# A key-value stack, code scalings and running sums: one DMA pass, five GpSimd steps and three VectorE steps put elsewhere in the order

## The reference

```python
# cross attention, on the layer-normed x; the first 257 context rows have weights of their own
q = rms_norm(linear(x, q_w, q_b), norm_q_w)
k = rms_norm(linear(context, k_w, k_b), norm_k_w)      # all further context rows
v = linear(context, v_w, v_b)
probs = softmax(einsum('bqhd,bkhd->bhqk', q, k) * scale)
out = linear(einsum('bhqk,bkhd->bqhd', probs, v), o_w, o_b)
# self attention: every weight is a product of codes and block scales
w = codes * jnp.repeat(scales, 32, axis=0)
```

## Time and profile before

| | us |
|---|---|
| median of 3 runs | 1200.07 (1199.26 to 1204.12) |
| the profiled execution | 1197.79 |
| its span, first to last instruction | 1196.1 |

### The profile page before, as it was taken

How to read it: one execution, slowest core, us unless ns; L and a number is a source line. 1 busy time by engine, 2 the same in 40 slices (tenths; PEclk the granted TensorE clock), 3 DMA queues, 4 the chain that set the end, 5 groups by cost and what they waited for, 6 DMA issues and landing times.

```text
span 1196.1 us, 26329 instructions
## 1 busy us (share of the span) xinstructions
PE 1154.2 (96%) x8794; PEld 950.5 (79%) x8794; DVE 947.6 (79%) x1611; ACT 876.7 (73%) x1891; POOL 764.0 (64%) x1064
## 2 busy tenths in 40 slices
PE   6999999999999999999999999999998879899998
PEld 4778888888888888888888888888887658588886
DVE  4778788887788787787878887778887778499997
ACT  5577877778777777777787777877777757388885
POOL 7988788887889788898887887888873000000000
PEclk9999999999999999999999999999999989899999
DMA  7135677665875657766667665686654899579990
GB/s 257 40 97 153 170 194 184 175 180 158 215 191 152 171 168 204 195 168 175 177 170 195 181 172 167 170 209 166 184 140 108 252 394 398 208 270 362 364 369 15
DMA packets 129327, 236.72 MB, mean 198 GB/s; under 512 B 15014, under 2 KB 42150, under 8 KB 128812
## 3 DMA queue, kind: packets, MB, share of 16 engines
q1 hardware_dynamic: 129196, 235.05, 66.5%
HBM read 140.87 MB, written 17.04 MB: 132 GB/s over the span
## 4 chain that ended last, share of the span: by engine, by line
PE 61%; POOL 11%; SPq 11%; DVE 6%; DMA 4%; issue 4%; ACT 2%; POOLq 0%; DVEq 0%; ACTq 0%
PE ps L1573 22%; PE ps L1437 12%; SPq L354 10%; PE ps L1599 5%; PE ps L1632 4%; DMA code_scale<-code_scales 3%; PE ps L1800 3%; PE ps L1803 3%; PE ps L1806 3%; POOL cx_blocks L624 2%; DVE small L1197 2%; POOL cx_blocks L622 2%; PE ps L1821 1%; PE ps L1829 1%; PE ps L1825 1%
## 5 line engine op out<-in xcount | busy, mean ns | idle before, releaser
L1573 PE MATMUL ps<-w_text,cx_blocks 128*128 128x512 f32 x1974 | 488.2, 394 | 0.5 <-ACT v_first L814 0.5
L1573 PEld LDWEIGHTS ps<-w_text,cx_blocks 128*128 128x128 f32 x1974 | 366.9, 188 | 86.8 <-issue 7.7
L857 ACT ACTIVATE p<-ps,small 128x512 f32<-128x512 f32 (+2 forms) x400 | 272.3, 682 | 116.7 <-DVE small L1199 112.8
L1197 DVE TENSOR_REDUCE small<-ps 128x1 f32<-128x512 f32 (+2 forms) x400 | 269.7, 674 | 87.4 <-PE ps L1599 86.9
L1437 PE MATMUL ps<-ident,p 128*128 128x128 f32 x1584 | 209.0, 273 | 11.0 <-DVE pt L1191 7.0
L1437 PEld LDWEIGHTS ps<-ident,p 128*128 128x128 f32 x1584 | 184.8, 141 | 41.2 <-issue 11.5
L839 ACT ACTIVATE pt<-ps 128x512 f32<-128x512 f32 (+1 forms) x296 | 164.4, 589 | 36.9 <-PE ps L1437 36.8
L622 POOL TENSOR_TENSOR cx_blocks<-cx_sum,small 128x256 fp32r<-128x256 f32 x188 | 119.1, 633 | 82.5 <-PE ps L1573 69.0
L624 POOL TENSOR_TENSOR cx_blocks<-cx_sum,cx_blocks 128x256 fp32r<-128x256 f32 x188 | 140.3, 746 | 14.7
L1599 PE MATMUL ps<-k_stack,q_stack 96*128 96x512 f32 (+1 forms) x400 | 146.2, 438 | 2.0 <-ACT p L857 1.7
L1199 DVE TENSOR_TENSOR small<-small 128x1 f32<-128x1 f32 x400 | 132.6, 331 | 13.7
(11 more groups left out here) (252 smaller groups left out, 1923.3 us busy)
## 6 DMA issues: line engine op xcount, KB each, us to landing
expert<-experts SPq DMA_DIRECT2D x34, 1536.0 KB, 8.7
k_stack<-kt_hi SPq DMA_DIRECT2D x384, 128.0 KB, 3.3
cx<-ctx_t SPq DMA_DIRECT2D x48, 512.0 KB, 5.0
k_stack<-kt_lo SPq DMA_DIRECT2D x192, 128.0 KB, 3.1
codes<-codes SPq DMA_DIRECT2D x64, 256.0 KB, 3.1
code_scale<-code_scales SPq DMA_DIRECT2D x64, 256.0 KB, 3.8
scaled<-codes SPq DMA_DIRECT2D x64, 256.0 KB, 2.3
weight_q<-scaled SPq DMA_DIRECT2D x1, 4096.0 KB, 15.3
```

Of the source, the lines that this page charges most:

```text
L857: eng.activation(pb[:, lo:hi], score_bank(s, h)[:, lo:hi], exp, bias=nm[1 - par][:, h:h + 1], accum_out=ls[1 - par][:, h:h + 1]).then_inc( ...
L1197: eng.tensor_reduce(ngm[:, h:h + 1], score_bank(s, h)[:, lo:hi], AX.X, ALU.max, negate=True).then_inc(e_gm, 1)
L1573: last = eng.matmul(ps_a[(p + i + 1) % 2][:, :], blk[:, i, a, c * P:(c + 1) * P], w_t[:, i, w, c * D:(c + 1) * D], start=(i in FRESH and c ...
```

## The change

- SyncE: the pass for tile C stands behind `stack(0)` instead of ahead of the load and `stack(0)`. In step 23 the last store moves with it; the wait for all stores stays behind it.
- GpSimd: scaling A comes after the third sum and block 4 of the first half, instead of ahead of them; scaling B after blocks 0 and 1 of the second half and the next group's first key norm, instead of ahead; scaling C at the end of the second half, instead of behind block 2. `key_norm(s, 3)` comes between the first and the second sum of the second half, instead of after both.
- VectorE: `scale_attention` is cut in two. In steps 2 to 23 the two steps on the sums run at the end of slot 1 and the rescaling at the end of slot 2, instead of both in slot 5. In the drained steps both stay where they were.

Nothing is added or removed.

```diff
@@ SyncE, step
-                pass_codes(s, 1, m, loop)
                 if 1 <= s < NG:
                     load_next(s)
                     eng.wait_ge(e_klo, s * GT + GT)
...
                     stack(0, False)
                     if not loop and s == NG - 1:
                         eng.dma_start(x_again[:, :], t["x"]).then_inc(e_xa, 16)
+                pass_codes(s, 1, m, loop)
                 if not loop and s == NG - 2:
                     for b in range(2):
                         eng.wait_ge(e_cs[b], 16 * (NW // 2))
@@ GpSimd, step
                 if strass:
                     split(0, 2, sum_y[:, :, :], 2)
                     split(0, 3, sum_x[:, :, :], 0)
+                    third_sum(0)
+                    split(0, 4, sum_x[:, :, :], 3)
                 scale_codes(s * W_STEP - (W_FIRST * W_STEP + 1), (m + 1) % 2, loop)
                 if strass:
-                    third_sum(0)
-                    split(0, 4, sum_x[:, :, :], 3)
                     fourth_sum(0)
                 if strass:
                     split(0, 5, sum_y[:, :, :], 4)
                 if nxt:
-                    first_sums(1)
+                    first_sum(1)
                 if cur:
                     key_norm(s, 3, 1)
+                if nxt:
+                    second_sum(1)
                 if strass:
                     split(0, 6, quarter(0, 1, 1), 0)
-                scale_codes(s * W_STEP - W_FIRST * W_STEP, m % 2, loop)
                 if nxt:
                     split_first(1)
                     if s > 0:
                         key_norm(s + 1, 0, 1)
                     if s == 0:
                         last_weight_sum()
+                scale_codes(s * W_STEP - W_FIRST * W_STEP, m % 2, loop)
+                if nxt:
                     split(1, 2, sum_y[:, :, :], 2)
-                scale_codes(s * W_STEP - (W_FIRST * W_STEP - 1), (m + 1) % 2, loop)
-                if nxt:
                     split(1, 3, sum_x[:, :, :], 0)
...
                     split(1, 6, quarter(1, 1, 1), 0)
+                scale_codes(s * W_STEP - (W_FIRST * W_STEP - 1), (m + 1) % 2, loop)
                 if s == NG - 1:
                     image_part()
@@ VectorE, slot and drain
-                    if end and j == 5:
+                    if end and s < NG - 1 and j == 1:
+                        scale_sums()
+                    if end and s < NG - 1 and j == 2:
                         scale_attention()
...
                     if end and h == 12:
+                        scale_sums()
                         scale_attention()
```

More of the change, by code:

```diff
@@ L629, in step @@
                 if strass:
-                    first_sums(0)
+                    first_sum(0)
+                    second_sum(0)
                 if cur:
```

6 lines of the change are left out of this document (4 added, 2 removed).

## The result

The changed kernel takes 1226.67 us, the median of 4 runs (1222.94 to 1232.08). Four runs of the kernel before on the same chip have a median of 1199.66 us (1198.69 to 1204.12). The ratio is 1.0221 with a 95% interval of 1.0175 to 1.0267: the kernel became 2.2% slower, where 0.5% faster was forecast. The profiled execution took 1226.28 us with a span of 1224.6, 28.5 more than before.

The account below looks back on a forecast made before the run. TensorE, busy 96% of the span, was taken as the bound, with 11.6 us lost in steps 2 to 23. 4.9 (key norm) + 3.4 (slot 7) - 0.4 (stack) - 2.0 (step 23) = 5.9 us off 1200.1: 1194.2 us, range 1190 to 1204.

Parts of the forecast that it names:

- the two places of loss: TensorE, steps 2 to 23: between slots 4 and 5 6.9 us lost, in slot 7 3.7 us.
- No more than that is to be had: Steps 2 to 23 take 811.1 us; 22 quickest steps would take 799.5, so at most 11.6 us can be gained.
- Slot 7: TensorE's slot 7, late in eight steps through VectorE's work in slot 5: moving that work gains 3.4 of 3.7 us.
- The third tile's landing: Tile C's scales land 2.9 us (1.9 to 4.5) after the origin, the start of the step's first score products.
- 17.1 us from the scaling to norm 3: GpSimd's stretch from the third scaling to the end of key tile 3's norm: 17.1 us, ending 20.0 after the origin.
- The bound of 21.7 for the norm: Key tile 3's norm on GpSimd costs nothing while it ends by about 21.7 us after the step's origin.
- Norm 1: GpSimd's key norm 1 ends near 6.5 us after the origin, ScalarE wants it at 7.5: covered by 1 us.
- doesn't do what it says: Rival: third tile lands 5 us or more after the origin, norm ends at 22.1, costs as before; 1199 us, chance 0.09.
- The stack: Second half of the key stack, behind SyncE's moved pass, delays ScalarE's copy in slot 2: 0.4 us over all steps.
- the rival's 12.6: Stack rival: second half lands over 11.9 us after origin, TensorE stands in slot 3; 12.6 us lost, 1207 us, chance 0.16.
- Step 23: SyncE waits for the last store's landing before the rows and the stack's second half: 2.0 us (0 to 3) lost.
- VectorE's cover: VectorE's idle waits in slots 1 and 2 cover the moved sums (about 0.8 us) and rescaling (0.68 us).

Follow-up runs that it names:

- the best kernel: Kernel before with VectorE's part, key norm 3 and scaling A moved, three row loads in step 24, loads ahead of store in each pass: 1186.98 us, ratio 0.9884.

## Why the prediction was wrong, point by point

- **What bounds the kernel.** TensorE's slots and the two places of loss were read rightly. "No more than that is to be had" was right too: the best kernel's steps take 36.37. What wasn't read is that the loss behind slot 4 came from a ring with next to no slack: GpSimd stood for the scales, and the scales were issued behind a stack that had waited for the norm of the step before. The prediction followed this chain for one step and stopped at the origin.
- **Slot 7.** 3.4 of 3.7 us were to go. It was right: slot 7 takes 4.09 in all of the 22 steps. But taken alone the part is worth nothing (1.0029).
- **The third tile's landing: the term that failed.** Predicted 2.9 after the origin, from an issue at -1.0 and a median landing of 3.8. Measured 5.85: the issue at 0.17, since the first half begins 9.0 and not 9.7 us ahead of the origin, and a landing of 5.63. The first miss is one of sign: the half ended 1.6 us ahead of the origin, and an origin that comes sooner after it makes that less; the prediction made it 2.0. (By its own terms, too, -1.0 + 3.8 is 2.8.) The median of all 64 passes was taken for the one that now stood behind a full queue, with a store of 256 KB ahead of it; the range's 4.5 was too low as well. With the loads ahead of the store it landed at 2.9, and the kernel took 1196.3 us against a forecast of 1194.2. That shows the rest of GpSimd's working to be sound.
- **17.1 us from the scaling to norm 3.** Measured 17.38, of which 0.4 is VectorE's rescaling. **The bound of 21.7 for the norm** held: at 21.0 nothing is lost, at 23.3 it costs 15.1 us more than before.
- **Norm 1** was covered "and gone if the tile lands at 4". It landed at 5.85, the norm ended at 9.5, and ScalarE stood for norms 68.8 us. The condition was named, but not its price.
- **The rival "doesn't do what it says"** had exactly this mechanism, a landing of 5 or more, at a chance of 0.09 and 1199 us. The price was too low as it took the norm at 22.1 and "costs what it did"; by its own formula 5.85 + 17.1 is 23.0, and late norms feed the next step's issue.
- **The stack.** Taken at 0.4 us; slots 2 and 3 lost 13.5, close to the rival's 12.6. The second half landed at 11.8 on average, by the rival's threshold of 11.9. Part of the 13.5 is norm 1 in front of the copy on ScalarE's queue, and part the lower clock in step 18; without norm 1 11.3 us stay, shown by scaling C in the next step. ScalarE's waits for the stack were 13.6 us in 14 cases, inside the 10 to 20 forecast, which shows that this sign was a poor one: the copy's lateness was booked to the norm.
- **Step 23.** Predicted 2.0 (0 to 3), measured 5.0 for step 24. The late second half took 2.2 of them, near the 2.0; the other 2.8 are the lower clock, which the prediction had nowhere.
- **VectorE's cover.** The 0.68 us of the rescaling were covered on VectorE's own timeline. On GpSimd's they cost 0.4 us a step, and without them there the changed kernel is 9 to 11 us faster in the medians, of which the profiles show 2 to 5 in the 22 steps.

The two rivals that spoke against the change did not exclude each other, and both came true; the prediction priced each alone.

## What to carry to other kernels

Where an engine waits for a DMA once a step, follow the chain on past the step's start until it returns to itself, and write its length beside the bound engine's step: if the ring has no slack, a gain elsewhere gives nothing, and every microsecond put into it is paid in every step. A load on which such a ring hangs is issued ahead of stores and ahead of bulk, and its landing is read from the passes that have the same neighbours in the queue, not from the median of all. A covered instruction is covered only if the engines that share its memory are idle as well. And before a longer slot is booked to a wait, its granted clock is read: part of the length can be the clock's.

## What the runs showed of the hardware that was not expected

The same 256 KB of scales, on the same queue, land in these average times: 3.3 us between the stack's halves with only its codes directly ahead, 5.6 there with a store of 256 KB directly ahead of both, 4.6 behind 24 stack DMAs, the load and the same store. In the last place the store ahead made no difference (4.57 with it, 4.61 without). Why a store matters only in the one place was not tried.

SyncE needs 0.60 us to issue one stack DMA, but some take 1 us and more, the longest of each kernel 1.9 to 2.2. One is in this pair in step 9 of the kernel before, which had one of its two longest intervals behind slot 4 in the step after:

```profile
378.02 2.37 SPq L354 DMA_DIRECT2D k_stack<-kt_hi  x2
```

The usual pair takes 1.24. What delays such an issue stays open.

TensorE's clock can fall to its lower level behind a single stand in a stream that is otherwise dense. It fell after stands of 1.97 and 1.95 us (changed kernel, steps 18 and 24), 2.24 and 2.02 (VectorE's part alone, steps 3 and 19), and 2.81 with 0.93 right behind it (SyncE's order as before, step 10). It did not after 2.10 in step 24 of the kernel with the last store ahead. So a wait can cost more than its own length, and whether it does differs from one execution to the next: 2.8 us of step 24 came and went in this way.
